# Another order for the aggregation, maxima, exponents and conversions in the edge steps of a graph kernel

## What is computed

```python
h = relu(layernorm(x))
node_att = softmax(h @ node_w, axis=0)
hh = h @ edge_w
e = where(adj > 0, hh @ hh.T, NEG_BIG)
output = (adj * (node_att * softmax(e, axis=1))) @ (h @ weight)
x = x + output + bias
h = relu(layernorm(x))
x = x + L1(h, adj, W)      # hyperbolic layer: two weighted sums over neighbours, tanh and artanh of norms
```

## Time and profile before

| what | us |
|---|---|
| median of 3 executions | 711.59 |
| lowest and highest of them | 710.37, 720.1 |
| the profiled execution | 714.95 |
| its span in the trace | 713.2 |

### The profile page before, as it was taken

The page is one execution under the profiler, slowest core; times in us unless marked ns, Lnnn a source line. Parts: engine busy times, 40 slices in busy tenths (PEclk is TensorE's granted clock), DMA queues, the critical chain, the costliest instruction groups (busy, mean ns, idle before and its releaser), DMA issues.

```text
span 713.2 us, 12464 instructions
## 1 busy us (share of the span) xinstructions
PE 495.1 (69%) x3804; PEld 416.4 (58%) x3804; DVE 478.2 (67%) x1977; ACT 351.1 (49%) x718; POOL 388.6 (54%) x458
## 2 busy tenths in 40 slices
PE   3697573749688777967877877987267587665750
PEld 2476442638688666866776767876245465544540
DVE  3486868887878768776887667777524354466774
ACT  2597765655564755526431465386412122234454
POOL 4053527274671736647575730038277777777752
PEclk9889866959999896978979899999669889999995
DMA  8955599986768886786232320001543334335632
GB/s 303 397 199 185 170 370 382 346 314 213 294 218 304 287 312 227 257 324 216 79 95 72 104 61 1 1 1 57 190 106 105 105 104 103 108 107 134 197 96 91
DMA packets 38166, 129.00 MB, mean 181 GB/s; under 512 B 6224, under 2 KB 23504, under 8 KB 34000
## 3 DMA queue, kind: packets, MB, share of 16 engines
q1 hardware_dynamic: 22736, 84.87, 31.5%
q0 software_dynamic: 15360, 43.29, 22.1%
HBM read 115.49 MB, written 12.65 MB: 180 GB/s over the span
## 4 chain that ended last, share of the span: by engine, by line
PE 28%; DVE 23%; POOL 16%; issue 12%; ACT 7%; DVEq 5%; DMA 5%; SPq 2%; POOLq 1%; ACTq 1%
POOL work L1486 10%; PE bank L815 10%; POOL work L709 5%; PE bank L754 3%; DVE fs L1049 3%; PE bank L864 3%; DMA work<-table_h,work 2%; PE bank L786 2%; PE bank L240 2%; PE bank L1768 2%; DMA table_h<-front 2%; PE bank L1585 2%; DVEq L1204 2%; DVE gx L1537 1%; DVE front L1066 1%
## 5 line engine op out<-in xcount | busy, mean ns | idle before, releaser
L709 POOL DMA_INDIRECT work<-table_h,work x160 | 160.0, 1000 | 74.1 <-issue 67.2
L609 ACT ACTIVATE work<-work 128x2048 bf16<-128x2048 f32 x64 | 121.8, 1903 | 59.6 <-issue 23.7
L1486 POOL DMA_INDIRECT work<-table_y,idx x128 | 124.3, 971 | 39.0 <-issue 38.1
L815 PE MATMUL bank<-work 128*128 128x128 f32 x640 | 102.6, 327 | 19.2 <-DVEq L1095 19.2
L815 PEld LDWEIGHTS bank<-work 128*128 128x128 f32 x640 | 96.6, 239 | 21.1 <-DVEq L1095 18.5
L1585 PE MATMUL bank<-work 128*128 128x257 f32 x256 | 75.5, 446 | 36.1 <-DMA work<-table_y,idx 36.0
L1585 PEld LDWEIGHTS bank<-work 128*128 128x128 f32 x256 | 53.8, 219 | 55.3 <-DMA work<-table_y,idx 47.1
L754 PE MATMUL bank<-work 128*128 128x256 bf16 x512 | 69.6, 292 | 0.0
L1049 DVE CUSTOM_DVE_ANT_0 fs<-work,bank 128x256 f32<-128x256 f32 x160 | 56.4, 417 | 11.8 <-DMA work<-table_h,work 6.1
L1614 ACT ACTIVATE work<-bank 128x257 f32<-128x257 f32 x32 | 12.2, 382 | 100.9 <-PE bank L1585 100.9
L1351 DVE SCALAR_TENSOR_TENSOR fs<-work 128x256 f32<-128x256 f32 x32 | 13.6, 426 | 71.2 <-ACTq L1615 70.6
(11 more groups left out here) (271 smaller groups left out, 1017.6 us busy)
## 6 DMA issues: line engine op xcount, KB each, us to landing
work<-in_adj SPq DMA_DIRECT2D x32, 2048.0 KB, 9.6
table_y<-work SPq DMA_DIRECT2D x8, 520.0 KB, 4.3
gx<-in_x SPq DMA_DIRECT2D x8, 512.0 KB, 8.5
table_h<-front SPq DMA_DIRECT2D x8, 512.0 KB, 4.4
front<-in_x POOLq DMA_DIRECT2D x8, 512.0 KB, 6.9
out<-gx SPq DMA_DIRECT2D x8, 512.0 KB, 3.2
work<-table_h,work POOLq DMA_INDIRECT x160, 3.6
work<-table_y,idx POOLq DMA_INDIRECT x128, 2.8
```

Source lines behind the costliest of these rows:

```text
L609: a.activation(abf[:, u % HALVES, :], adu[:, b % 2, h, :], ACT.Copy, accum_out=cnt[:, k, b, h:h + 1]).then_inc(L["conv"], 1)
L709: p.indirect_dma_start(gat[:, k, n, :], None, table_h, bass.IndirectOffsetOnAxis(ix[:, k, n:n + 1], 0)) \
L815: last = t.matmul(bank[4 + b % 2][:, c * P:(c + 1) * P], gat[:, k, n, c * P:(c + 1) * P], otp[:, n, :], start=(q == 0), stop=(q == TILES - 1))
L1486: p.indirect_dma_start(gtm[:, n % OCT, q, :], None, table_y, bass.IndirectOffsetOnAxis(idx[:, n * TILES + q:n * TILES + q + 1], 0)) \
```

## The change

Nothing is added or dropped but one drain: the same instructions stand in another order on three engines. On TensorE, the aggregation of block 2 is moved ahead of the sums by slot, the aggregation of block 3 stays behind them, the expansion of the row maxima comes ahead of the two projections, and the fourth transposition comes behind the look-up of the edge words. On ScalarE, conversion unit 2 of the group ahead is moved up between the two aggregates, ahead of the softmax exponents; unit 3 stays behind these. On VectorE, the subtraction of the maxima (now `less`) is moved from `weights` into `edge_list`, ahead of the second round of maxima (into `body` behind `row_max` where there is no `wd`), the reciprocal and its product go behind L1093, and the last three instructions of `edge_list` become `edge_words`, behind `weights`.

```diff
                 conv(0, ahead)
                 conv(1, ahead)
-                for b in (2, 3):
-                    aggregate(b)
+                aggregate(2)
+                conv(2, ahead)
+                aggregate(3)
                 if at_:
...
-                conv(2, ahead)
                 conv(3, ahead)
...
-                for b in range(GB):
+                for b in range(GB - 1):
                     ott(b)
-                    if b < GB - 1:
-                        aggregate(b // 2, b % 2)
+                    aggregate(b // 2, b % 2)
...
+                ott(GB - 1)
                 aggregate(1, 1)
...
                 pack(7)
+                for c in range(KD):
+                    aggregate(2, c)
                 if at_:
                     g, k = at_
                     t.wait_ge(L["ohe"], g + 1)
...
                     last.then_inc(L["es"], 1)
-                for b in (2, 3):
-                    for c in range(KD):
-                        aggregate(b, c)
-                proj(2)
-                proj(3)
+                for c in range(KD):
+                    aggregate(3, c)
...
                     last.then_inc(L["mx"], 1)
+                proj(2)
+                proj(3)
...
+        def less(d, g, k):
+
+            d.wait_ge(L["mx"], g + 1)
+            d.tensor_reduce(ee[:, 1, :], bank[3][:, 0:4 * GT].rearrange("p (n s) -> p n s", s=4)[:, :, 0:3],
+                            AX, ALU.add)
+            d.drain()
+            d.tensor_tensor(ee[:, 1, :], ee[:, 0, :], ee[:, 1, :], ALU.subtract)
+            d.drain().then_inc(L["less"], 1)
...
                     d.match_replace(e48[:, b, :], s16[:, b, 0:8], e48[:, b, :], -1.0)
                 d.drain()
+                if at_:
+                    less(d, *at_)
...
             def weights(g, k):
...
-                d.drain().then_inc(L["less"], 1)
                 d.wait_ge(L["agg"], GB * g + 2 * GB)
                 d.wait_ge(L["pexp"], g + 1)
...
                 d.drain().then_inc(L["otp"], 1)
+                d.wait_ge(L["den"], g + 1)
+                then(d, d.reciprocal(sm[:, 4, :], sm[:, 2, :]))
+                d.tensor_tensor(sm[:, 3, :], sm[:, 4, :], natt[:, grp(g)], ALU.mult)
...
                     row_max(*at_)
+                    less(d, *at_)
...
                     weights(*at_)
+                if wd:
+                    edge_words(d, *wd)
```

More of the change, by code:

```diff
@@ L936, in beside @@
                     edge_list(d, 0, 0, None)
+                    edge_words(d, 0, 0)
             return beside
+        def less(d, g, k):
[5 more added lines that the diff above has]
+            d.drain().then_inc(L["less"], 1)
         def edge_list(d, g, k, at_):
@@ L988, in edge_list, with edge_words @@
                 d.drain().then_inc(L["nv"], 1)
+        def edge_words(d, g, k):
+                ti, tw = ia.bitcast(I32), ib.bitcast(I32)
                 d.tensor_tensor(sm[:, 5, :], alpha[:, grp(g)], nv[:, k, :], ALU.not_equal)
@@ L1082, in weights @@
             def weights(g, k):
-                d.wait_ge(L["den"], g + 1)
-                d.reciprocal(sm[:, 4, :], sm[:, 2, :])
-                d.wait_ge(L["mx"], g + 1)
-                then(d, d.tensor_reduce(ee[:, 1, :], bank[3][:, 0:4 * GT].rearrange("p (n s) -> p n s", s=4)[:, :, 0:3],
-                                        AX, ALU.add))
-                d.tensor_tensor(ee[:, 1, :], ee[:, 0, :], ee[:, 1, :], ALU.subtract)
-                d.tensor_tensor(sm[:, 3, :], sm[:, 4, :], natt[:, grp(g)], ALU.mult)
-                d.drain().then_inc(L["less"], 1)
                 d.wait_ge(L["agg"], GB * g + 2 * GB)
```

## The result

| what | before | after |
|---|---|---|
| median of 13 executions each, us | 712.01 | 707.45 |
| lowest and highest | 707.64, 720.1 | 695.87, 715.95 |
| the profiled execution | 714.95 | 706.16 |
| its span | 713.2 | 704.4 |
| ratio after to before, 95% interval | | 0.9843 [0.9803, 0.9882] |

By the ratio the kernel is 1.6% faster, by the medians 0.6%; the ratio compares only executions within 1.5% of each kernel's fastest, and of the changed kernel these are five of thirteen. Its times fall into two groups, four from 695.87 to 699.34 and nine from 706.16 to 715.95. The profile is of the shortest of the second group. The forecast was 704.6 in a range from 697.5 to 712.0, and "within 2%" had 0.87.

What follows compares the result with a forecast made beforehand. Two loops meeting at the dot products bound it: GpSimd with its DMAs, and TensorE, VectorE, ScalarE. The latter's 5.4 us plus 2.3 from x loads minus 0.8 for clock gave 6.9: 704.6 us, range 697.5 to 712.0.

Steps and rivals of the forecast that it cites:

- within 2%: Predicted chance, 0.87, that a measurement tells no change; 2% is about 14.2 us; faster had 0.10, slower 0.03.
- The two loops: Edge steps: loop A and B meet at VectorE's dot products; B's gain before step 6 is lost unless A speeds up.
- loop A: GpSimd and its DMAs in the edge steps: 20 gathers, x load, wait, bias; 46.0 us from one bias to the next.
- The x loads: GpSimd's four x waits beside adjacency loads: adjacency loads moving ahead cut their sum from 41.3 to 39, 2.3 us saved.
- B: Loop of TensorE, VectorE and ScalarE in the edge steps, rearranged by the change; 1.4 to 3.2 us gained per `wd` step.
- B after the meeting: Steps 6 to 9: gains of 3.2, 1.4 and 0.9 us; with 0.1 net lost at the end, 5.4 us.
- Steps 8 and 9: Steps without `wd`: statistics queued behind `less` eat the gain of the early `mx`; 0.1 us gained in each.
- The clock: TensorE at step ends: longer idling puts more first aggregations at the low clock, 0.8 us lost over three steps.
- After step 9: VectorE behind L1093 of step 9: the reciprocal and its product delay the last statistics by some 0.2 us.
- Loop A holds everything: Rival, no change: last gathers land late, dot products end hardly earlier; 2 us gained, 709.5 us; chance 0.13.
- Loop A moves up with B: Rival, faster: the four x waits fall to 8 us each; about 13 us gained, 698.5 us; chance 0.18.
- The slower rivals: Each of four x waits 13.35 us: 717.6 us, chance 0.08; `mx` blocking VectorE every step: 711 us, chance 0.05.

Runs made afterwards that it cites:

- the early x load: GpSimd issues its x load ahead of the eleventh gather instead of behind the twentieth: in the changed kernel 694.55 us, in the kernel before 708.81 us.

## Why the prediction came out as it did

**Direction and size.** Forecast 6.9 us for the profiled execution, measured 8.8; the median lies 2.9 us above the forecast. That is closer than the terms deserve, as several were wrong with opposite signs.

**The two loops.** Right, and shown: moving one DMA issue of loop A by ten gathers brings the last new x 16.3 us forward between the two profiled executions, and another 12.9 us off the median. Wrong was where they meet. I took the meeting at 307.10, in step 6, to be pulled ahead by the 2.3 us saved on x. But loop A was 0.4 us late at its first x load (127.16 against 126.81), 1.5 at the second and 1.2 to 3.3 from there to the fourth, gathers landed 1.1 us slower at the median, and the scores of step 6 came 1.4 us later. This step of the working missed by 3.7 us.

**The x loads.** Their sum is 37.6 us, forecast 39, and inside 35 to 45. The step that failed is its reason, adjacency loads that move ahead with B against x loads that stay. Three waits kept their sum, and one fell by 3.7 because the adjacency load came 5.8 us later than before, not earlier, and so behind the x load: B was held up by loop A. That the sum of the four came near the forecast is luck. The Trainium skill, page "DMA: Bandwidth & Descriptors", section "Queues, rings and completion order", has each DMA engine take turns between queues packet by packet, and the prediction concluded from it that who is issued first matters little. The three waits at 33.35 against 33.31 fit that; the fourth doesn't: issued 1.2 us ahead of the adjacency load instead of 3.4 behind it, it fell from 7.98 to 4.25, as short as the loads with no adjacency load near.

**B after the meeting.** Forecast 3.2 + 1.4 + 0.9 = 5.5; from the scores of step 6 to those of step 9 it is 5.2, as 2.2 + 1.9 + 1.1, so the first term was 1.0 too large and the other two too small. The mechanism showed as foretold: the multiplication directly behind the new x, the aggregation ahead of the sums, the 1.52 us wait gone.

**Steps 8 and 9.** Forecast 0.1 each; from scores to multiplication they gained 1.4 and 1.5. The step that failed is `mx` at 8.3 us behind the dot products (430.7 against 422.4). It came 7.0 behind them (425.5 against 418.5). I had put all of the first aggregation, 2.9 us, into the path to the sums. It starts at 418.69, while VectorE still prepares the scores until 421.0, and the sums start at 421.08. And each half was 2.47, not 2.9 to 3.2. So `less` waited 1.15 us and not 2.5, and the queue behind it was released earlier. That this queue costs something was right: 1.0 us a step, as measured on the second chip.

**The clock.** Forecast as a loss of 0.8, and it was a gain on the whole: all 640 records of the aggregation together took 100.6 us instead of 102.6. The loss exists: at the start of step 7 the stretch from the first aggregation to the look-up takes 6.94 us (327.98 to 334.92) instead of 6.50, though one transposition fewer lies in it; over steps 4 to 8 these stretches sum to 31.0 us instead of 30.6. But the filled wait gives back 0.9 to 2.5 us of aggregation in steps 3 and 6 to 9 (4.9 us against 5.9 to 7.35), and takes 0.8 and 0.4 in steps 4 and 5. The Trainium skill, page "TensorE: Matmul & The Clock Gate", section "What's actually happening", calls the throttled clock the default that activity lifts; I had noted that by this rule the filled wait would give some back and then took the loss alone. The windows agree with it, 0.56 before and 1.00 after, and 0.50 where the filling was undone. How much of these records' time reached the span is shown only for steps 8 and 9, where VectorE waits for the maxima behind them.

**After step 9.** Forecast a loss of 0.2; gained 1.4 in step 10 and 2.1 in the second layer. TensorE in step 10, the projections and aggregation of its middle, after:

```profile
441.49 1.13 PE L786 MATMUL bank<-w,front 128*128 128x256 f32 x4 [1.10 <-ACT front L649]
442.46 4.63 PE L815 MATMUL bank<-work 128*128 128x128 f32 x40
```

Before they took 1.99 and 5.47 us: 1.7 us of clock again. The first aggregation of step 10 went the other way, 6.33 us behind 4.32 of idling instead of 4.70 behind 2.15, but only 0.3 us of that reached the projections, as TensorE had stood 1.63 us for a copy there before. Among the six profiles at this speed the second layer took between 255.5 and 261.8 us without being touched, so its 2.1 us are no effect that can be put down to the change.

**The rivals.** "Loop A holds everything" is what the profiled execution shows up to step 5, and not beyond. "Loop A moves up with B", 698.5, isn't what the profiled execution shows, yet four executions took 695.87 to 699.34. Since the early x load leaves no time above 700.5, it is likely that these four are executions in which the x loads came quickly; no profile of one was taken, so that stays argued. The slower rivals had nothing for them: the x waits summed to 37.6, and `mx` blocked nothing in steps with `wd`. In steps without `wd` it costs 1.06 and 1.15 us of waiting, and 5.77 and 4.52 where the filling is missing.

**What stays open.** The single worth of the early conversion and of the look-up on the first chip; the cause of the two groups of times (TensorE's mean granted clock isn't it: 0.852 to 0.867 in the lower group, 0.854 to 0.878 in the upper); why the first two x loads of loop A came later and the wait behind the second was 1.6 us longer.

The best kernel by median is the changed one with the early x load, 694.55 us, 0.9811 [0.9768, 0.9853] of the time before.

## What to carry to other kernels

Find the loops that meet, and ask of each part of a reordering which loop it shortens: the reordering of loop B was worth 4.6 us of median (1.6% by the ratio) with loop A's x load at the end of the gathers, and 14.3 us (708.81 to 694.55) with it in their middle. Work put into an idle stretch of TensorE can pay twice, by its own length and by the clock of what follows; here it did so in five of seven steps. When a wait is moved ahead of other work, check first that what it waits for was moved ahead as well: with it 0.6% to 1.6% faster here, without it 1.35% slower.

## What the runs showed of the hardware

- The same 40 records of aggregation took 4.9 us where TensorE was granted 1.00 throughout and 5.9 to 7.35 where part of them ran at the 1.2 GHz level. The length of the idling alone doesn't order them. In one piece, behind the wait and the small matmuls of the sums: 6.34 after 1.66 us idle (granted 0.73 over them, the kernel before with the early x load), 5.89 after 3.00 (0.79), 6.18 after 3.71 (0.75), 7.10 after 5.12 (0.65). In two halves with the first directly behind the wait: 4.95 after 2.96 and after 1.31 (1.00), 7.09 after 5.06 (0.50 over the first half).
- GpSimd stood 3.6 to 4.3 us for a 512 KB x load with no adjacency load ahead of it and 8.0 to 13.6 where 2 MB adjacency loads were under way; the second of the four (13.35, 13.24, 13.61, 13.57 us in four kernels) was always the worst.
- The same kernel took 712 us on one chip and 879 and 884 on two others, where 16% to 18% of the chain was a releaser outside the profile's view.
